# Node stages of a graph network: the issue offsets of SyncE's loads and stores

## What is computed

```python
h = jnp.maximum(_layernorm(x, axis=-1), 0.0)
x = x + _L0_gnn_ref(h, ...)   # relation-typed messages: agg + h @ self_loop_weight + bias, relu
h = jnp.maximum(_layernorm(x, axis=-1), 0.0)
x = x + _L1_gnn_ref(h, ...)   # 4-head edge attention, exp, segment sums, divided by the sum of weights
h = jnp.maximum(_layernorm(x, axis=-1), 0.0)
x = x + _L2_gnn_ref(h, ...)   # SAGE twice: h @ W_self.T + mean(neighbours) @ W_neigh.T + bias, layer norm
h = jnp.maximum(_layernorm(x, axis=-1), 0.0)
x = x + _L3_gnn_ref(h, ...)   # GCN: normalised sum over neighbours and self, h @ W
```

## Time and profile before

| | us |
|---|---|
| median of 3 runs (lowest 3520.6, highest 3520.91) | 3520.66 |
| profiled execution: time | 3522.34 |
| profiled execution: span from first to last instruction | 3520.6 |
| node stage REL, first sum load to last store | 529 to 843 |
| node stage SAGE0 | 2037 to 2335 |
| node stage SAGE1 | 2604 to 2956 |
| node stage GCN | 3228 to 3521 |

### The profile page before, as it was taken

One profiled execution on the slowest core, in us unless ns is written; L12 is line 12 of the kernel. 1 busy time (PEld: TensorE's weight loads), 2 busy tenths in 40 slices (PEclk: granted clock), 3 DMA queues, 4 the chain that ended last, 5 costly groups with the idle time before them and its releaser, 6 DMA issues. The chain is left out here.

```text
span 3520.6 us, 67545 instructions
## 1 busy us (share of the span) xinstructions
PE 2423.8 (69%) x14044; PEld 1902.6 (54%) x14044; DVE 2450.3 (70%) x10828; ACT 1709.5 (49%) x4561; POOL 2583.7 (73%) x2869
## 2 busy tenths in 40 slices
PE   5988878995656656600069877756678885666898
PEld 3444437774655555500058855545566664555777
DVE  6787879995645455458856678753448887556898
ACT  2333327885544444401134477731136664556787
POOL 5777757777888888755577788857779893777885
PEclk9999999998877777755556689865579997557999
DMA  7355539995333333368822279952249995223998
GB/s 265 129 210 215 212 129 294 313 310 171 69 60 62 62 59 63 55 190 283 275 68 52 52 249 314 302 185 52 52 150 347 335 343 189 52 52 113 313 317 289
DMA packets 328242, 638.58 MB, mean 181 GB/s; under 512 B 61072, under 2 KB 89776, under 8 KB 321992
## 3 DMA queue, kind: packets, MB, share of 16 engines
q1 hardware_dynamic: 233406, 501.99, 42.3%
q0 software_dynamic: 90944, 133.85, 16.0%
q10 hardware_dynamic: 3786, 1.65, 0.2%
HBM read 371.35 MB, written 277.50 MB: 184 GB/s over the span
## 5 line engine op out<-in xcount | busy, mean ns | idle before, releaser
L795 POOL DMA_INDIRECT got<-rows,gidx x588 | 603.8, 1027 | 236.3 <-issue 168.1
L851 POOL DMA_INDIRECT sums<-parked,tidx x588 | 601.0, 1022 | 107.6 <-POOL tidx L840 92.7
L1129 ACT ACTIVATE n_h<-ring 128x128 f32<-128x128 f32 x1176 | 484.1, 482 | 170.2 <-issue 117.7
L1408 PE MATMUL bank<-edge_cells,ident 128*128 128x128 f32 x2352 | 459.9, 278 | 0.0
L1275 PE MATMUL bank<-parked 128*128 128x512 f32 x784 | 369.2, 614 | 53.1 <-DVE parked L1667 46.6
L1265 PE MATMUL bank<-ident,edge_cells 128*128 128x128 f32 x588 | 137.5, 378 | 378.5 <-ACT edge_cells L996 377.8
L865 POOL DMA_INDIRECT attsums<-ring,sidx x196 | 312.7, 1595 | 78.7 <-issue 63.3
L1408 PEld LDWEIGHTS bank<-edge_cells,ident 128*128 128x128 f32 x2352 | 362.1, 194 | 0.0
L1405 PE MATMUL bank<-w_t,n_ht 128*128 128x128 f32 x1568 | 291.0, 301 | 62.7 <-DMA edge_cells<-sums 62.6
L1559 DVE COPY gidx<-src_i 128x4 int32 (+1 forms) x225 | 44.0, 196 | 407.4 <-DMA got<-rows,gidx 201.0
L1265 PEld LDWEIGHTS bank<-ident,edge_cells 128*128 128x128 f32 x588 | 94.4, 190 | 425.6 <-ACT edge_cells L996 354.7
(11 more groups left out here) (191 smaller groups left out, 6489.3 us busy)
## 6 DMA issues: line engine op xcount, KB each, us to landing
edge_cells<-sums SPq DMA_DIRECT2D x392, 264.0 KB
ring<-rows SPq DMA_DIRECT2D x343, 264.0 KB
rows<-ring SPq DMA_DIRECT2D x294, 264.0 KB
edge_cells<-attsums SPq DMA_DIRECT2D x98, 264.0 KB
rowsg<-ring SPq DMA_DIRECT2D x98, 264.0 KB
ring<-rowsg SPq DMA_DIRECT2D x98, 264.0 KB
sums<-parked SPq DMA_DIRECT2D x16, 1584.0 KB
attsums<-parked SPq DMA_DIRECT2D x16, 1584.0 KB
```

Source lines behind the costliest of these rows:

```text
L795: pool.indirect_dma_start(out=got[:, b, j, 0:width], out_offset=None, in_=table[:, :], in_offset=bass.IndirectOffsetOnAxis(ap=gidx[:, b, j ...
L851: pool.indirect_dma_start(out=sums[:, :], out_offset=bass.IndirectOffsetOnAxis(ap=tidx[:, t % 16:t % 16 + 1], axis=0), in_=parked[:, t, :] ...
L1129: last = nc.scalar.activation(n_h[:, b, k, :], x_data(phase, g)[:, k, :], ACT.Relu, bias=x_col(phase, g, k, COL_C), scale=x_col(phase, g, ...
L1408: last = nc.tensor.matmul(o, lhsT=ident[:, :], rhs=s_rows(phase, g)[:, k, 0:D], start=False, stop=(bias is None or k == K - 1))
```

## The change

In the node stages REL, SAGE0 and GCN the lag of the sum load goes up by three (2 to 5) and the store's lag by three as well (9 to 12; 7 to 10 in GCN). In SAGE1 the lag of the sum load goes from 3 to 4, that of the residual load from 5 to 4, the store keeps 10. The order within a turn becomes x, residual, sums, store. ATT is as before (its `load_x2` does nothing). No engine but SP has another list.

```diff
-                s_lag = {REL: 2, ATT: 0, SAGE0: 2, SAGE1: 3, GCN: 2}[phase]
-                store_lag = {REL: 9, ATT: 6, SAGE0: 9, SAGE1: 10, GCN: 7}[phase]
-                stages = [(load_x, 0), (load_s, s_lag), (load_x2, 5), (store, store_lag)]
+                s_lag = {REL: 5, ATT: 0, SAGE0: 5, SAGE1: 4, GCN: 5}[phase]
+                store_lag = {REL: 12, ATT: 6, SAGE0: 12, SAGE1: 10, GCN: 10}[phase]
+                stages = [(load_x, 0), (load_x2, 4), (load_s, s_lag), (store, store_lag)]
                 if phase == REL:
                     stages.append((row_stored, store_lag + 2))
                 run_steps(sp, stages, GROUPS, SLOTS, behind=SLOTS)
```

## The result

The changed kernel takes **3589.01 us** (median of 4 runs, 3586.71 to 3597.1). The kernel before, run beside it, takes 3520.78 us (3520.6 to 3524.31). That is 68.2 us more, a ratio of 1.020 with a 95% interval of 1.0188 to 1.0212. The profiled execution of after took 3588.72 us (before 3522.34), its span is 3587.0 us (before 3520.6), and its mean granted clock is 0.799 (before 0.804).

A forecast was written before the change was run, and what follows sets the result against it. SP's own issuing was taken as the pace in SAGE1 and GCN, DVE in REL. SAGE1 +41, GCN +10, REL +3 and SAGE0 -3 gave +51 us on 3520.66: 3572 us, range 3535 to 3618.

The forecast's parts named there:

- SP was the pace before: SAGE1 and GCN: SP goes from issue to issue, hardly waiting for compute, at 3.46 us a group in SAGE1.
- A ring over three groups: SAGE1: row ready, SP's store and loads, sums land, PE, DVE's statistics; 8.13 + L us over three turns.
- L: Landing time of the sum load, issue to PE's first product; taken as 3.6 us in SAGE1.
- the upper rival: Landing stays as long as in the loaded stage: SAGE1 4.26 us a group, +72 us, some 3620 us in all; chance 0.15.
- The size in SAGE1, +41 us: SAGE1 slows to 3.91 us a group, 0.45 us more over 90 groups; bounds +14 and +72 us.
- PE's product to the statistics: SAGE1: time from PE's first product of a group to DVE's statistics, taken as 2.09 us.
- rival 2: Landing falls towards 2.7 us: SAGE1 +14 us, the rest near 0, 3535 us in all; chance 0.11.
- The residual load's wait for its store is covered: SAGE1: the store was issued some 5 us before, enough for landings of 3.6 to 4.7 us.
- GCN, +10 us: GCN: input load waits for row g-8 with sums of g-5 behind; 3.01 us a group, bounds -3 and +29 us.
- REL, +3 us: REL: input load waits for the add of g-8, mostly covered by DVE's own work; bounds 0 and +10 us.
- SAGE0, -3 us: SAGE0: inputs get three groups further ahead and ACT's 50.7 us of waits go; bounds -10 and 0 us.
- my signs of being wrong: L718 in SAGE1 hardly waits, sums' lead stays above 4.6 us, or edge stages change by over 2 us.

The follow-up runs named there:

- The second read: SP reads the due number twice in SAGE1, added to the kernel before (3563.49 us) and to the changed kernel (3605.81 us), each against 3520.9 us.
- the ring open: The changed kernel with SAGE1's store lag 10 to 11 and its residual load at lag 5: 3525.34 us against 3517.38 for the kernel before.

## Why the prediction came out right, point by point

- **SP was the pace before.** Right. The second read costs its full length there (0.58 us a turn), and a shorter or rarer read gains 11 to 23 us in SAGE1.
- **A ring over three groups binds SAGE1 after.** Right, by three signs: the sum load's lag alone gives the whole loss, one more turn for the store takes it all back, and an addition to SP's turn costs a third of its length. That the ring closes did not by itself give the time: L had to be chosen, and the rows left it between 2.7 and 4.66 us. My choice gave 3.91 us a group, 0.14 below the pace of after, and the upper rival's gave 4.26, 0.21 above it.
- **The size in SAGE1, +41 us, was short: it is +52.3.** I had 11.73 us for the lap (8.13 + 3.6) and 3.91 us a group. The means over groups 14 to 83 of after are 0.18 us from row ready to store, 0.65 to the input load, 1.90 to the sum load, 4.05 to the first product, 2.36 to the statistics and 3.08 for DVE's part, 12.22 us in all. A third of it is 4.07, and the pace of those groups is 4.05. SP's part came out 0.23 us shorter than its 2.96 us, since the read got shorter behind the residual load. Two terms were too small. The **landing L** is 4.05 us and not 3.6. I had argued that less traffic brings it near SAGE0's row. The share did fall to 0.87, as forecast, and below SAGE0's 0.92, but L fell only from 4.67 to 4.05. Part of the error is that SAGE0's 3.66 was one group's: in the kernel before, the 29 of groups 14 to 83 of SAGE0 in which DVE stood waiting for sums have 3.87 us in the mean. Part of it is that L runs to PE's first product and so holds PE's own lateness: in the 52 groups of after in which PE stood waiting it is 3.92 us, in the other 18 it is 4.43. **PE's product to the statistics** is 2.36 us and not 2.09. There the granted clock fell from 0.96 to 0.91 over the stage, and PE runs part of its work at the lower of its two levels, as two transposes of one shape in this stage of after show:

```profile
2803.98 0.60 PE L1381 MATMUL bank<-ident,ring 128*128 128x128 f32 x4
...
2812.35 1.06 PE L1381 MATMUL bank<-ident,ring 128*128 128x128 f32 x4
```

 The second one comes after PE had waited 1.81 us for sums. At 1.2 GHz instead of 2.4 it takes 1.06 us instead of 0.60. The windows before and around it show the granted clock:

```profile
2803.00:2810.70 7.70, 5.69 (x45) 4.76 (x44) 6.83 (x28) 4.71 (x16) 6.91 (x11) 1.00 0.92 294
2810.70:2814.40 3.70, 3.70 (x18) 2.93 (x17) 1.80 (x10) 0.87 (x2) 3.28 (x6) 0.54 0.96 339
```

 In 50 of groups 14 to 83 the clock stayed at full speed from the first product to the statistics, and this time is 2.14 us in the mean. In the other 20 it is 2.90 us; before, there were 4 such groups. So some 0.22 of the 0.27 us lie in the groups with the lower clock. In a ring such a wait may feed on itself; that is not shown.
- **The landing figure of the Trainium skill** ("DMA: Bandwidth & Descriptors", section on the anatomy of one DMA) would have given 2.6 us and 3.58 us a group. That section fits it to DMAs issued by GpSimd, which my text left out; the loads here are SyncE's. The row from a quiet stretch, 2.7 us, agrees with it. The trace of after has 4.05 us for L and 4.05 us a group, so rival 2, a landing near 2.7 us, did not come. The 12 residual loads of SAGE1 whose landing stands in this trace took 4.4 us in the median.
- **The residual load's wait for its store is covered.** Right in the changed kernel, where this wait does not appear among SP's waits. With the ring open it does appear, 23.4 us in 31 waits, at the faster pace of 3.35. So the cover is the slow pace of the ring.
- **GCN, +10 us: it is +8.4.** I had 3.01 us a group; it is 2.99. (The terms ahead of L add up to 5.19 us, not 5.1, which with L = 3.9 is 3.03 a group.) From the sum load's issue to the finished row are 7.21 us in the median, and my terms gave 3.9 + 1.96 + 1.13 + 0.2 = 7.2 us. The input load now stands waiting for its row (issue 0.17 us after it, before 4.14) and the sums are asked for 4.28 us ahead of their use instead of 7.80.
- **REL, +3 us: it is +0.7.** The input load waits for L1870, 73 times, but DVE stays full (301.42 of 315 us), and the pace is 3.02 against 3.06. Sums asked for 5.03 us ahead instead of 13.0 were still early enough. The sum had a small cost in it; the measured one is near the lower bound, 0.
- **SAGE0, -3 us: it is -1.2**, which is within its variation. ACT's waits for inputs are gone, as this row of ACT in SAGE0 of after shows (busy us, mean ns, idle us before):

```profile
L1129 ACT ACTIVATE n_h<-ring 128x128 f32<-128x128 f32 x380 | 155.5, 482 | 0.0
```

 And nothing came of it, since what is late next is the sums: DVE waited for them 34.4 us in 37 waits before (L1904), and now 44.5 us in 50. An engine's 50 us of waits were worth nothing here.
- **The missed term: ATT's edge stage, +5.7 us.** A change of more than 2 us in an edge stage was one of my signs of being wrong, and it came. I followed the store's lag through SP's own list and left out `row_stored`, which signals POOL. A store that goes out three turns later puts POOL's fetches behind, and ATT's first gather with them. The kernel with only REL's store moved shows it.
- **What was to be seen.** SAGE1 stage of some 390 us: it is 403.4. DMA share near 0.87: it is 0.87. GCN's L670 waits for L1955 where L718 did: 50 times. L718 waiting in most of 98 groups by half a us: it is 72 waits of 1.5 us on average. The wait is as frequent as I had said and longer.

The forecast of 3572 us was 51 us above the median of before, and the profiled executions differ by 66.4. Of the 15.4 us between them 11.3 are SAGE1, 5.7 ATT's edge stage, 1.8 SAGE0, and REL and GCN give back 2.3 and 1.6; the other stages make up 0.5.

**What stays open.** Why a read of `due_i` takes 0.8 us right behind an input load and 0.28 to 0.35 us behind a residual load, a store or another read. A DMA's issue just ahead of it does not explain it alone, since the residual load and the store are such issues too. No run changed the granted clock in SAGE1's ring, so its share of the loss is read from one trace only.

Why SAGE0 does not gain from shorter or rarer reads can be read in part. Its sum loads wait until POOL has said that the scatter has come far enough (L837 before, L838 in the kernel with a read at every other group). These waits in SAGE0, before and then in that kernel:

```profile
SPq L697 <- POOLq L837: 20.4, 14, 3.1
SPq L698 <- POOLq L838: 54.7, 34, 6.3
```

The time that SP was spared went into waiting for POOL. What sets POOL's own pace there was not followed up.

## What to carry to other kernels

When a queue runs in order, do not ask how far ahead of compute an issue is. Look for the instruction in the queue that waits for a result, and count how many groups lie between that result and the one the next load behind it feeds: the time of the lap over that count is a floor for the pace, and one group more or less decides its sign (SAGE1's store at lag 10 or 11, GCN's sums at 5 or 4). Where the issuing queue is itself the pace, its small steps (a register read of 0.8 us that becomes 0.28 us in another place) can be worth more than the distance of a prefetch, as they were here. And follow each signal that a moved instruction gives, also to engines that the change does not name.

## What the runs showed of the hardware

- **The time of a register read on SP depends on its place.** Medians of 807 ns right behind the input load, 354 ns behind the residual load, 290 ns behind another read, and 282 ns behind the store, all in the same stretch of SAGE1. The Trainium skill gives a floor of about 600 ns for it ("DMA: Bandwidth & Descriptors", section on latency and other measured facts). The rows here go down to 262 ns.
- **A DMA share of 1.0 is not a ceiling.** SAGE1 ran at 1.01 and 341 GB/s before, and at 1.04 and 379 GB/s with half the reads left out.
- **Landings of 264 KB loads follow the traffic only in part.** From issue to first use in SAGE1, means over groups 14 to 83: 4.67 us at a DMA share of 0.96 (before) and 4.05 us at 0.87 (after), but 4.37 us at 0.97 (only the residual load moved) and 3.93 us at 0.90 (second read before). In a quiet stretch a load took 2.7 us to land.
